# Pairs of tiles and cells in the first layer of a graph network: a 256-column stationary one-hot and a 512-column moving one

## The reference, cut to what matters

```python
msg = relu(x[src] + edge_attr @ We + be)                 # layer 0
h = x + segment_sum(msg, dst)                            #   then a small MLP and a batch norm
out = segment_sum(h[src] * dinv[src] * dinv[dst], dst)   # layer 1, twice
agg = segment_sum(transformed[etype, src], dst)          # layer 2, twice
for _ in range(10):                                      # layer 3
    out = segment_sum(out[col] * w, row) * 0.9 + h * 0.1
```

## Time and profile before

| | |
|---|---|
| three timed runs | 7447.78, 7451.00, 7455.83 us, median 7451.0 us |
| profiled execution, span | 8461.5 us |
| PE busy | 5291.4 us, 63% |
| PEld busy | 4245.3 us, 50% |
| DVE busy | 2665.6 us, 32% |
| ACT busy | 1602.0 us, 19% |
| POOL busy | 3312.3 us, 39% |
| DMA | 914.46 MB in 532,598 packets |

### The profile page before, as it was taken

How to read it: one execution, slowest core, us unless ns; L and a number is a source line. 1 busy time by engine, 2 the same in 40 slices (tenths; PEclk the granted TensorE clock), 3 DMA queues, 4 the chain that set the end, 5 groups by cost and what they waited for, 6 DMA issues and landing times.

```text
span 8461.5 us, 137122 instructions
## 1 busy us (share of the span) xinstructions
PE 5291.4 (63%) x43763; PEld 4245.3 (50%) x43764; DVE 2665.6 (32%) x6088; ACT 1602.0 (19%) x3471; POOL 3312.3 (39%) x3299
## 2 busy tenths in 40 slices
PE   3332332466666668884444445444445999999998
PEld 2111111233333338873333334333335999999998
DVE  5000001577767663232222222222223111111111
ACT  2221121013455641021111112111110000000000
POOL 2555556656555530006666654666661000000000
PEclk7655565578777788895665567666657999999999
DMA  6111111623333335442222243222225666666665
GB/s 256 47 46 42 48 45 47 70 60 79 82 82 90 87 52 179 141 151 63 64 64 62 71 67 120 71 64 71 64 60 127 200 198 198 200 198 198 200 198 164
DMA packets 532598, 914.46 MB, mean 108 GB/s; under 512 B 223705, under 2 KB 366058, under 8 KB 532254
## 3 DMA queue, kind: packets, MB, share of 16 engines
q1 hardware_dynamic: 285816, 621.27, 23.8%
q0 software_dynamic: 104896, 162.89, 9.4%
q10 hardware_dynamic: 141670, 128.06, 4.9%
HBM read 705.38 MB, written 205.67 MB: 108 GB/s over the span
## 4 chain that ended last, share of the span: by engine, by line
PE 48%; another core or an unknown queue 23%; issue 13%; DVE 7%; ACT 4%; DVEq 2%; POOL 1%; ACTq 1%; DMA 1%; POOLq 0%; SPq 0%
PE bank L1454 28%; PE bank L1319 4%; PE bank L1399 3%; PE bank L1308 2%; PE bank L1480 2%; PE bank L1161 2%; PE bank L1472 2%; PE bank L1431 2%; DVEq L1898 1%; ACT staged_records L912 1%; ACT own_term L901 1%; ACT staged_records L1083 1%; POOL rec_dst L771 1%; DVE rows L1867 1%
## 5 line engine op out<-in xcount | busy, mean ns | idle before, releaser
L786 POOL DMA_INDIRECT rows<-relation_table,staged_rows x1664 | 1642.8, 987 | 1652.0 <-DMA staged_rows<-table_rows_of_tiles 808.7
L1454 PE MATMUL bank<-own_term,h_transposed 128*128 128x192 f16 x16464 | 1379.1, 247 | 56.1 <-DMA h_transposed<-edge_counts_T 33.5
L1454 PEld LDWEIGHTS bank<-own_term,h_transposed 128*128 128x128 fp8e4 x16464 | 1365.7, 98 | 57.5 <-issue 56.6
L786 POOL DMA_INDIRECT rows<-node_table,records_in x832 | 880.1, 1058 | 695.8 <-PE bank L1308 408.7
L1454 PE MATMUL bank<-own_term,staged_records 128*128 128x192 f16 x12348 | 1032.4, 246 | 0.0
L1454 PEld LDWEIGHTS bank<-own_term,staged_records 128*128 128x128 fp8e4 x12348 | 1020.0, 98 | 0.0
L771 POOL DMA_INDIRECT rec_dst<-staged_records,staged_record_rows x781 | 771.4, 988 | 622.3 <-ACT staged_record_rows L921 387.0
L1399 PE MATMUL bank<-rows,onehot 128*128 128x96 f32 x3328 | 637.9, 351 | 494.4 <-issue 386.7
L1950 DVE TENSOR_TENSOR edge_sums<-edge_sums,bank 128x96 f32 x1664 | 421.4, 253 | 1542.6 <-PE bank L1399 638.1
L1399 PEld LDWEIGHTS bank<-rows,onehot 128*128 128x128 f32 x3328 | 574.7, 258 | 549.3 <-issue 538.8
L1472 PE MATMUL bank<-ident,staged_records 128*128 128x128 bf16 x2401 | 273.8, 276 | 806.2 <-ACT staged_records L1083 629.9
(11 more groups left out here) (346 smaller groups left out, 5311.7 us busy)
## 6 DMA issues: line engine op xcount, KB each, us to landing
h_transposed<-edge_counts SPq DMA_DIRECT2D x280, 784.0 KB, 4.2
staged_records<-edge_counts SPq DMA_DIRECT2D x210, 784.0 KB, 4.2
h_transposed<-edge_counts_T SPq DMA_DIRECT2D x56, 784.0 KB, 4.3
rec_dst<-records_in SPq DMA_DIRECT2D x80, 520.0 KB, 7.1
records_in<-rec_dst SPq DMA_DIRECT2D x104, 400.0 KB
edge_counts_T<-staged_records ACTq DMA_DIRECT2D x343, 112.0 KB
staged_records<-edge_counts_T ACTq DMA_DIRECT2D x49, 784.0 KB
edge_counts<-staged_records ACTq DMA_DIRECT2D x49, 784.0 KB
```

The source lines that it names most:

```text
L786: pool.indirect_dma_start(out=rows[:, g, j, 0:D], out_offset=None, in_=source, in_offset=at(ap=index(g, j), axis=0)).then_inc(gathered[g], 16)
L1454: last = nc.tensor.matmul(banks[j][:, 0:2 * D], slots[c][:, at:at + P], z[:, c * SB + i, :], start=(c == 0 and i == 0), stop=(c == SG - 1 ...
```

## The change

A pair's stationary one-hot gets 256 columns and its moving one-hot 512. Source blocks 0 to 3 of a group and blocks 4 to 6 now share columns of `code_oh`: column = (block in the group, less 4 if it is 4 or more) x 128 + target place. `place_oh` says which half is meant: columns 0 to 127 are the source places of edges from blocks 0 to 3, columns 128 to 255 those from blocks 4 to 6. The first matmul uses the first 128 stationary columns and all 512 moving columns, the second the other 128 and the first 384 moving columns. The cell's sums are now 896 columns in a row, 512 in one bank and 384 in the next.

So that a record can say its half, `sloc` is raised by 128 for edges from blocks 4 to 6, with one operation at the start and two ahead of the first `record_rows`. `src_col` is corrected for it in each of the three phases of the loop, with four operations where there were two. `place_no` gets a second half.

```diff
+LOW = 4
+CW = LOW * P
-        one_pair = (GC + P) * 2
+        one_pair = (CW + 2 * P) * 2
-        code_oh = [bytes_of(a, lo, GC, F16) for a, lo in ring]
-        place_oh = [bytes_of(a, lo + GC * 2, P, F16) for a, lo in ring]
+        code_oh = [bytes_of(a, lo, CW, F16) for a, lo in ring]
+        place_oh = [bytes_of(a, lo + CW * 2, 2 * P, F16) for a, lo in ring]
-        place_no = sb("place_no", [P, P], F16)
+        place_no = sb("place_no", [P, 2 * P], F16)
-        cell_sums = psum[:, :].rearrange("p (b n) -> p b n", n=BANK)
-        HALF = GC // 2
+        halves_of_cell = ((0, CW), (CW, GC))
...
-                    at = 2 * ((parity + g) % IN_FLIGHT)
-                    cell = cell_sums[:, at:at + 2, 0:HALF]
+                    at = 2 * BANK * ((parity + g) % IN_FLIGHT)
+                    cell = psum[:, at:at + GC]
...
-                    nc.scalar.copy(cell_st[g].rearrange("p (b n) -> p b n", n=HALF), cell,
-                                   saturate=False).then_inc(cell_kept, 1)
+                    nc.scalar.copy(cell_st[g], cell, saturate=False).then_inc(cell_kept, 1)
...
-                    for j in range(2):
-                        last = nc.tensor.matmul(psum[:, bass.ds(at[k] + j * BANK, HALF)], place_oh[i],
-                                                code_oh[i][:, j * HALF:(j + 1) * HALF], start=False, stop=True,
+                    for j, (lo, hi) in enumerate(halves_of_cell):
+                        last = nc.tensor.matmul(psum[:, bass.ds(at[k] + lo, hi - lo)], place_oh[i][:, j * P:(j + 1) * P],
+                                                code_oh[i][:, 0:hi - lo], start=False, stop=True,
                                                 skip_group_check=True)
...
-            then(V.tensor_scalar(high_t, high_t, 37.0, None, ALU.mult))
-            then(V.tensor_scalar(high_t, high_t, 8, None, ALU.logical_shift_right))
-            then(V.tensor_copy(grp, high_t))
+            then(V.tensor_scalar(low_t, high_t, 37.0, None, ALU.mult))
+            then(V.tensor_scalar(low_t, low_t, 8, None, ALU.logical_shift_right))
+            then(V.tensor_copy(grp, low_t))
+            then(V.scalar_tensor_tensor(blk_in, low_t, -float(SB), high_t, ALU.mult, ALU.add))
...
+            then(V.tensor_scalar(blk_in, blk_in, float(LOW), float(P), ALU.is_ge, ALU.mult))
+            then(V.tensor_tensor(sloc[:, :], sloc[:, :], blk_in, ALU.add))
             record_rows(0)
...
-            then(V.tensor_copy(place_no[:, :], places[:, 0:P]))
+            then(V.tensor_copy(place_no[:, 0:P], places[:, 0:P]))
+            then(V.tensor_scalar(place_no[:, P:2 * P], places[:, 0:P], float(P), None, ALU.add))
...
-                    V.tensor_scalar(code_oh[i], col_no[:, :], group_base[:, bass.ds(lo + k, 1)], src_col[:, bass.ds(t, 1)],
+                    V.tensor_scalar(code_oh[i], col_no[:, 0:CW], group_base[:, bass.ds(lo + k, 1)], src_col[:, bass.ds(t, 1)],
                                     ALU.add, ALU.is_equal)
...
-                then(V.scalar_tensor_tensor(src_col[:, lo:hi], word[0], float(P), word[2].bitcast(F32), ALU.mult, ALU.add))
-                then(V.scalar_tensor_tensor(src_col[:, lo:hi], word[3].bitcast(F32), -float(P * NB), src_col[:, lo:hi],
-                                            ALU.mult, ALU.add))
+                place = word[3].bitcast(F32)
+                then(V.tensor_scalar(src_col[:, lo:hi], place, float(P), float(P * P * NB - CW), ALU.is_gt, ALU.mult))
+                then(V.tensor_tensor(src_col[:, lo:hi], src_col[:, lo:hi], word[2].bitcast(F32), ALU.add))
+                then(V.scalar_tensor_tensor(src_col[:, lo:hi], place, -float(P * NB), src_col[:, lo:hi], ALU.mult, ALU.add))
+                then(V.scalar_tensor_tensor(src_col[:, lo:hi], word[0], float(P), src_col[:, lo:hi], ALU.mult, ALU.add))
```

3 lines of the change are left out of this document (2 added, 1 removed).

## The result

The changed kernel takes 7442.01 us at the median of 20 runs (7435.09 to 7446.67), the kernel before 7455.37 us (7447.32 to 7462.86, 20 runs) beside it. The ratio is 0.9984 with an interval of 0.9977 to 0.999: faster by 13 us, 0.16%. The forecast was a gain of 22 us. The measured gain lies 2 us short of the near edge of the forecast's own range of 15 to 60 us. It is the outcome that the prediction called "within 0.2%", to which it gave a chance of 0.38, most of it for the rival in which nothing is gained.

A forecast was written before the change was run, and what follows sets the result against it. The prediction took a ring of waits to bound the first layer's loop, with DVE, PE and POOL nearly equal. Its terms, -26 us from PE's waits and +4 us setup, gave -22 us: 7451 to 7429 us, range 7385 to 7460.

The forecast's parts named there:

- within 0.2%: Outcome for the whole kernel: a difference of at most 15 us, not told from no change; chance 0.38.
- The price per column: DVE's two one-hots: 0.26 ns a column, 256 columns fewer, so 67 ns a pair and 77 us over 1152 pairs.
- the slower rival: Place one-hot's 0.16 us doubles, 0.06 us more a pair; 7490 to 7524 us, deciding from 0.26 us; chance 0.10.
- PE and ACT unchanged: Pair matmuls stay at 896 columns and 10.74 us a slot; ACT's copy and check keep their time; difference nothing.
- The setup, +4 us: Added operations at the start and in the three phases, plus the second half of `place_no`: +4 us (1 to 6).
- What reaches the path: First layer's loop: DVE's saving counts only at PE's 86 one-hot waits, 0.4 us each, 34 us; three quarters taken, 26 us.
- three loops nearly equal: In a first-layer slot without gaps, DVE needs 10.82 us, PE 10.74 and POOL 10.0.
- the stretches: First layer's loop: profile-only periods with register instructions taking about 700 ns, put at 446 us and left out of the reckoning.
- PE's sequencer sets the slot: Rival in the first layer's loop: PE's register work fixes 10.74 us a slot, nothing gained, 7455 us; chance 0.36.
- DVE sets every slot: Rival in the first layer's loop: slots fall from 10.82 to 10.02 us, all 77 us gained, 7378 us; chance 0.12.

The follow-up runs named there:

- a_dve_less: The changed kernel with the code one-hot computed for 128 columns instead of 512, PE reading these repeatedly so its work stays; ratio 0.997 to the kernel before.
- a_dve_as_before: The changed kernel with the code one-hot made 768 columns wide instead of 512, the extra 256 unread by PE; ratio 0.9996 to the kernel before.

## Why the prediction was right in sign and short in size

**The price per column was right.** Forecast: 0.26 ns a column, code step 0.43 to 0.33, place step 0.16 to 0.19, 67 ns a pair. Found, where nothing disturbs: 0.42 to 0.32 and 0.16 to between 0.19 and 0.20. The width of 128 columns in `a_dve_less` lies on the same line: (0.32 - 0.23) / 384 = 0.23 ns. The doubled place one-hot did not double, so the slower rival never came near its point of 0.26 us. The estimate of 67 ns a pair that the prediction worked out from the VectorE page of the Trainium skill (VectorE: DVE Perf Modes, The TRN2 errata) is borne out by these steps: 0.10 us less on the one and 0.03 to 0.04 more on the other.

**PE and ACT unchanged: right.** PE's pair matmuls were 605.8 us and are 612.6, ACT's check 1009 and 1008 ns, its copy 917 and 916.

**The setup, +4 us: right as far as it can be seen.** L1928 and L1929, the two added operations of the three phases, took 0.38 to 0.50 and 0.51 to 0.85 us each, about 3 us in all against 2.7; the second half of `place_no` 0.23 against 0.25. From the first target one-hot of the first layer to the first slot with pairs it is 61.3 us, where it was 58.8.

**What reaches the path: the step that was off.** The term was 86 waits at 0.4 us, three quarters of it, 26 us. The stage gave 15. PE's waits for one-hots did fall by 18 us, from 200 to 182, but not where the time was gained: in the first 48 slots they fell by 5.5 us and the slots by 10.5, in the others by 13 and 4.8. That a part of DVE's saving would reach the end was right; which part, and why, was not, and that the sum came near is in part luck. Three things were wrong in it.

The first is who sets the slot. The prediction had three loops nearly equal, with PE's at 10.74 us from the earlier trace rows, and took DVE's saving to count only at 86 waits of PE. But PE's 10.74 us was DVE's pace seen at PE. Six sequencer instructions less on PE moved no ordinary slot, six more only one of three, by 0.21 us. DVE set them in the kernel before and sets them in the changed one, with its datapath and in places, by the spacing, with its own sequencer. The prediction had the register operations of L1898 in the earlier trace rows and used them as a sign of the stretches only; it counted PE's sequencer per pair and not DVE's. It also took all that a slot has over 10.8 us for stretches, 446 us; the stretches were 302, and the rest is the fourth slots of about 13 us and the slots of the second half, which average 13 us (610.2 / 47).

The second is what is left of 0.80 us in an ordinary slot. These are the sums of the twelve code steps and the twelve place steps of a slot, start to start on the timelines, means over the slots of the first 48 without other waits:

| slot of the body | before: code, place | changed: code, place |
|---|---|---|
| first | 5.27, 2.04 | 4.68, 2.35 |
| second | 5.27, 2.09 | 4.54, 2.38 |
| third | 5.13, 2.30 | 4.28, 2.83 |
| undisturbed steps x 12 | 5.04, 1.92 | 3.84, 2.34 |

The last row is the forecast, 0.78 us less. In the first two slots of a body the place steps are as forecast, but the code steps are 0.7 to 0.8 us over their undisturbed sum, where the kernel before had 0.23 us. In the third the code steps are 0.44 us over and the place steps 0.49. Of these 0.49 the step from the first pair to the second has 0.34, which had 0.24 in the kernel before, and the four behind it have 0.04 to 0.05 each, which is the 0.57 us of the first six pairs. So the saving is lost twice: mostly to code one-hots of 0.50 to 0.62 us, and by about 0.2 us in one slot of four to the spacing that I put down to the sequencer.

What makes the code one-hots long stands in the timelines: of 576 in the first 48 slots 193 took over 0.45 us, and in each of these one of POOL's gathers ends. Of the 383 others it ends in 78, and only starts in 159. Those wholly inside a gather, 126, took 0.42 us at most. In the kernel before 77 of 576 took over 0.55 us, where the others take 0.50 at the mean, and a gather ends in each of the 77 too. In the slot shown POOL's gathers of 1733.09 (0.98 us) and 1734.38 (0.94 us) end inside the two long ones. No run here takes the gathers away, so that they cause it is argued, not shown.

The SBUF page of the Trainium skill (SBUF — State Buffer, SBUF: two separate sides) says that VectorE in its two-port modes and GpSimd share a port pair as an exclusive lock, where the later one is blocked for the whole instruction. The trace has lengthened one-hots beside POOL's gathers, but nothing of a whole instruction's length: the longest is 0.22 us over the usual 0.40, and the other 383 code one-hots stay at 0.40 to 0.45 us, though a gather is under way 0.95 us out of every 1.25.

The third is that slots are of three kinds. In the first 48, the 36 ordinary ones brought in 13.3 us, 0.37 each, and the twelve fourth ones took 2.8 us back, 0.23 each. In the 47 slots of the second half DVE's saving is slack: it waits 82 us for PE before `edge_sums`, 9 more than before, and of the 4.8 us that came in `a_dve_as_before` ties only 1.1 to DVE's columns.

**The rivals.** "PE's sequencer sets the slot" (0.36) is right in part for the second half, where ACT is on the path too, and wrong for the first; its 7455 us with no gain is ruled out by the interval. "DVE sets every slot" (0.12) had the right engine in the first half, but neither its rate nor the second half. Both are nearer to what was found than the forecast's own account by PE's waits. By what is known now, its term should have been 36 x 0.37 - 12 x 0.23 = 10.5 us in the first half and little in the second.

The trace page of the Trainium skill (Perfetto Trace Analysis, Sequencer Loop) was weighed for PE alone. It tells of every engine's sequencer that control instructions are executed by it in microcode and engine instructions are queued, and so of DVE's. The trace fits it: 0.57 us a pair in places, with 512 columns and with 128.

**What stays open.** How the second half is shared between PE's sequencer and ACT: more on either lengthens it (17 us for about 0.9 us a slot on PE, 10 for about 1.0 us on ACT), less on PE shortens it, and less on ACT was not tried. Why the sequencer's pause behind a branch is 2.8 us in some rounds and 3.3 in others. Whether the long code one-hots are POOL's doing, and why the wider ones of the kernel before lost 0.23 us a slot to it and these 0.8. Why the twelve fourth slots got longer, and what gave the 3.7 us of the second half that did not go back with DVE's columns.
